# One core, a sequence layer with learned memory and routing: all steps of all stages in another order

## What is computed

```python
k, v, q = (causal_dwconv(hidden @ W.T, cw, cb) for W in (Wk, Wv, Wq))
alpha, eta, theta = gates(hidden)                       # one number each per token
for c0 in range(0, S, 128):                             # chunk by chunk
    g = grad(mem_loss)(W_state, k[c], v[c]) * 0.1       # pred = silu(k @ W1.T) @ W2.T
    g = g * min(1 / norm(g), 1)
    # per token: S = eta*S - theta*g;  W = (1-alpha)*W + S; W is kept for each token
    h = silu(q[c] @ W1t);  out[c] = h @ W2t
y = rmsnorm(out @ Wo.T) * norm_g * (hidden @ gW.T + gb)
x = layernorm(hidden + y)
x = layernorm(x + expert_w[argmax(x @ gate_w.T)] @ x)   # one of 8 experts per token
```

## Time and profile before

| | |
|---|---|
| median of 3 runs | 500.34 us (500.19 to 500.83) |
| span of the profiled execution | 498.6 us |
| PE busy | 435.3 us, 87% |
| weight loads of PE busy | 332.3 us, 67% |
| DVE busy | 392.7 us, 79% |
| ACT busy | 313.3 us, 63% |
| POOL busy | 274.6 us, 55% |
| mean granted clock of PE | 0.961 |

### The profile page before, as it was taken

One profiled execution on the slowest core, in us unless ns is written; L12 is line 12 of the kernel. 1 busy time (PEld: TensorE's weight loads), 2 busy tenths in 40 slices (PEclk: granted clock), 3 DMA queues, 4 the chain that ended last, 5 costly groups with the idle time before them and its releaser, 6 DMA issues.

```text
span 498.6 us, 11093 instructions
## 1 busy us (share of the span) xinstructions
PE 435.3 (87%) x3506; PEld 332.3 (67%) x3506; DVE 392.7 (79%) x1233; ACT 313.3 (63%) x791; POOL 274.6 (55%) x353
## 2 busy tenths in 40 slices
PE   6976999999999999899997989998679887996970
PEld 3654687767868677766866775866558776785750
...
GB/s 234 140 145 105 92 118 87 140 111 129 183 71 171 78 204 73 173 91 156 148 104 189 95 165 121 121 145 91 298 173 139 162 189 239 173 235 208 235 86 55
DMA packets 61353, 73.20 MB, mean 147 GB/s; under 512 B 17293, under 2 KB 48206, under 8 KB 61296
## 3 DMA queue, kind: packets, MB, share of 16 engines
...
## 4 chain that ended last, share of the span: by engine, by line
PE 35%; DMA 19%; DVE 16%; issue 10%; POOL 9%; ACT 9%; SPq 2%; POOLq 0%; DVEq 0%; ACTq 0%
DMA sorted_rows<-rows,index 7%; PE bank L523 6%; PE bank L624 5%; PE bank L1352 4%; DMA out<-os,xs_token 4%; POOL sorted_rows L1127 4%; ACT rows L1049 4%; DVE y L1007 3%; PE bank L544 3%; POOL index L1123 2%; DMA front<-sorted_rows 2%; DMA y<-in_hidden 2%; DVE kq_in L573 2%; ACT junk L990 2%; PE bank L1057 1%
## 5 line engine op out<-in xcount | busy, mean ns | idle before, releaser
L1127 POOL DMA_INDIRECT sorted_rows<-rows,index x64 | 77.0, 1203 | 27.0 <-issue 12.2
L1397 POOL DMA_INDIRECT out<-os,xs_token x71 | 70.1, 987 | 36.6 <-DVE mv L1026 14.1
L573 DVE SCALAR_TENSOR_TENSOR kq_in<-shared,conv_w,kq_in 128x256 f32<-128x256 f32 x144 | 60.7, 474 | 8.9 <-ACT kq_in L564 8.8
L523 PE MATMUL bank<-front 128*64 128x256 f32 x512 | 61.6, 394 | 6.8 <-DMA front<-in_w_kv 4.7
L624 PE MATMUL bank<-front 128*128 128x256 f32 x256 | 62.5, 388 | 0.7 <-DVE gt L629 0.7
L1352 PE MATMUL bank<-shared,front 128*128 x212 | 53.0, 394 | 5.3 <-ACT front L1331 1.8
L523 PEld LDWEIGHTS bank<-front 128*64 128x64 f32 x512 | 37.0, 141 | 26.5 <-DMA front<-in_hidden_t 5.7
L624 PEld LDWEIGHTS bank<-front 128*128 128x128 f32 x256 | 46.8, 193 | 8.8 <-issue 1.6
L1352 PEld LDWEIGHTS bank<-shared,front 128*128 128x128 f32 x212 | 39.4, 195 | 13.2 <-issue 8.5
L1049 ACT ACTIVATE rows<-y,rstd 128x256 f32<-128x256 f32 x64 | 34.0, 590 | 18.5 <-DMA sorted_rows<-rows,index 14.4
L1015 POOL DMA_DIRECT2D y<-in_hidden x16 | 16.1, 1007 | 35.7 <-DVE y L1007 27.8
...
## 6 DMA issues: line engine op xcount, KB each, us to landing
...
q<-kq_in SPq DMA_DIRECT2D x64, 64.0 KB, 2.9
...
hq<-hq SPq DMA_DIRECT2D x64, 64.0 KB, 2.6
shared<-in_w_expert SPq DMA_DIRECT2D x2, 1024.0 KB, 11.9
```

Source lines behind the costliest of these rows:

```text
L523: ins = pe.matmul(halves[half(side), kind, :, :], w[:, k, kind * D:(kind + 1) * D], pairs[:, k, side, :, :], start=k == 0, stop=k == KH - 1)
L573: dve.scalar_tensor_tensor(dst, raw[g][:, kind, :, tap:tap + P], conv_w[:, kind, tap:tap + 1], dst, ALU.mult, ALU.add))
L1127: pool.indirect_dma_start(sorted_rows[:, :], bass.IndirectOffsetOnAxis(index[i2][:, b:b + 1], 0), R[:, b, :], None, bounds_check=NE * REGI ...
L1397: pool.indirect_dma_start(out[:, :], bass.IndirectOffsetOnAxis(xs_token[t % LOADS][:, i:i + 1], 0), os_[o][:, i, :], None, bounds_check=TO ...
```

## The change

Only the text ORDER is another one. It has the same 2388 entries, each generator as often as before, in another sequence; products with the same cut of the array stand next to each other more often. No operation, buffer or wait is added or taken away. Of the text's lines, the first five and the three with the entries 1620 to 1799 (around the last projection, `pf`, and the load of the weights, `w0`):

```diff
 ORDER = (
-    "p0p0p0p0g0p1p0p0p0p0p0p0p0p0p0p0p0p1p0p0p0p1p0p0p0p1p0p1p0p0p1p1p1p1s0p1p1p1p1p1p1p1p1p1p1p1p0p1l0p0s0p1p1l0p2p0l0p1p1l0"
-    "p1p0l0s0p1s0s0l0s0s0p1l0s0l0l0s1l0s1p0p1l0l0s0l0s0l0l0l1p4s1l0l1s0l0s0p2p2s1p1p2p2p2p1l0s0p2p2s0p3s0p2p2s1p2p2p2s1p2p2p2"
-    "p2p2p2p2p2p1l1l1l1s0l0s2l0p2s1s1r0l1l1p2l1s2r0r0l1p2r0s2s1l1s2l1l1s1l1l1s1p2s2s1l2l1l1r0l1p2r0p3s2s2l1p3s2l2p3p3r0l1s1l1"
-    "p3s1r0p3p3p3s1l2p3p3p3p3p3p3p3p3p3p3p3p3l2r0p2p3p3l2r1s1l2l2p3e0s3l2r1l2r1e0p6e0p2p3p2e0s3p3l2l2s2e0l2e0l2e0s3r0r0s2e0l2"
-    "l2p3s2r1l2s3l3p3p3s2l3p4p3e0s3s3p4l2s2p4p4p4s2r1s2p5l2e0p4r1l3e0p4p4p4e0e0e0r1p4p4p4p4p4p4p4l3p4p3p4p4r0p4e0r1l3s3e0e0l3"
+    "p0p0p0p0p1p0g0p1p1p0p0p0p0p0p0p0p1p1p0p0p0p0p0p0p0p0p1p0p1p1p1p1p1p1p1l0l0p1p0p1l0p1p1p1p1p1p1p1p0p0p0p0s1l0l0p1p0l0s1p0"
+    "s0l0l0p1p0s0l0s1l0p1l0l0l0l0p1s0l0p1p1p1l1s0l0p3s0l1l0s0p2p2p2s1p1s0p2s0p2s0p2l0s1p2s0l1p2p2s0s0p2p2p2p4p2p2p2p2p2s1p2p2"
+    "p2l1p2l1s0p2s0p2p1p1p2l0p2l1s0l0l1p2p2l1l1p2r0l0l1l1s1p2l1r0l1l1s0s2l2s1l1s2s1s1s1l1r0s1s1r0l2r0r0p3p3p3l1p3s2l1l1l1p3p3"
+    "p3s2r0p3l2p3p3p3p3p3p3s1p3p3p3p3p3s2p3s1p3r1l2r0p3e0r1p3l2r1e0e0l2s1p3l2s3r1l2s3s2e0e0l2l2s2e0p3r0e0l2l2r0p3e0l2l2s3s2p3"
+    "s2l3p3e0p6r1r1s2p4s2l3r1l2l2p4s2p3l2s3p4p4e0e0p4p5l2e0p4e0e0p4p4l3e0p4p3p3s3p4r1p4p4p4p4p4p4r0p4p4p4l3s2s2p4l3e0s2e0s3r1"
 ...
-    "pfpfebpfecpeecrdseleebecpfrdpelepfpfealepfseealfebecebecececleecselfeasfebebserdebpfeblfserdleseebleebpfeblerdealepeleec"
-    "lfpfsfeapflfw0ebebealfebeblfebsfleebebebebpfrdebeblesfecpfy0y0sfy0pfeceby0rdecpfedecedecpfecpfley0ecebedy0edpfsfececlfec"
-    "ecy0leedlelfecsfeblflfededrerex0edlfeclfecedx0x0ecw0lfx1w0ecsfsfrex0sfecx1x1eclfx2sflfx2x1x2x2x0x3x1x1x2sfx3ededededx1ec"
+    "leebrdecpfpfeardrdeaeaecpfpfseebebrdeblepfeaebebpepflfecececececpflesepeecpflfseeaeblfpfebebebrdebseleebebseleleleebebrd"
+    "lesflfeblfeblfebebpfebpfrdebebleebebsflflfy0pfrdpelepfsflfsfecececy0ececy0sfebsflfpfpfrdpfecw0edlfecebebedy0y0pfecedy0pf"
+    "ecy0edlfleeclex0edececx0lex0reededx0lfedsfedw0ecececw0x1eclfedecx1sfreecsfsfx2rex1ecsfx2x2ecx1x2edecedecx0ececedx1x2x3x1"
 ...
```

More of the change, by code:

```diff
@@ L1429 @@
[L1429 to L1444, removed]
@@ L1453 @@
[L1453 to L1456, removed]
@@ new lines @@
+    "r1l2l2e0s2l3e0l3s4e0p4p4p4l3r1s3e0e0e0p4e0e0e0s3r1l3r2e0s4l3r0l3r2p4l3e0e0l3r2e1e0r0l3s3r2s3s3e1e1s4e1s3s4l4s4l3e0l3e1e1"
+    "l3e1e0l3l3r2r2e1s3p5p5p5l4l3p5e0p5r2p5p5e1p5p5l4p5p4p5p5s3e0p5p5p5e0l4s3p5p5p5p5l4s3p5r2p5l4s4p4r3r2p4e2e0l4s5p5l4l4e2e1"
+    "p5e1l4p5r3e2p5r1s4e1p5r3s5e1l4e1e0l4l4r1e0s4e0e1e2r3p5s5p5l4r2l4l5l5s4e1e1p7s4l4l4e1s4l4s4r2s5s4p6e1p5e1s4p6p6r2l5s5p6e2"
+    "p6l5s4p6p6p6p6r3e2e2e2e2p5p6p6r3p6p6p6p6p6r3p6p6p6p5l4p6s5l4p6e1e1p6e1l5p6e1l5p6s6l5l5l5e1p6r3r4r3e1s5r4r2l5e1l5r4s4e1l5"
@@ new lines @@
+    "l5r3l5s6e0s5e2r2e1e2l6e2e0e3l5e1e2e2l6r3s5e3l5e3s5r4p7e2s5e2p7e2e2s5e3l5e2e2s6r3l5e1s6s6p7l5e1l6s6p7r4e3r4e3l6l6e3e3s5e3"
+    "l6p7e2p7e1e2p7e1r4p6p7p8e1l5e1l6p7e2p7p9p7p7s6p7p7p7l6e1r3p7p7s5e2l6p6e1p7p7e2p7r5r3e2s5e1p7l6p7s5r4s7r5p7e3s7l6l6l6p7e2"
+    "r4e3p6r5r5l6p7e3e2e3e1e2e3s6p7p7p7s7p7e1s6r4e2e3s7e4r4l6e4s6s6e3l6r5e2s6s7r5p8e4r5s6e2e3e3e3s6e4r4e3p8e4l6e4p8e4l7p8e4p8"
+    "l7p7p8p8e2e2p7e3l6p8s6l6l7e2p8s7p8l6e2p8p8e4e3e3p8p8s7l7e2p8p8p8p8e2p8p8p8p8p8r5l7s7r6l7e3e3r6l7l7r6s7e3l7p8r5p8e2e3r5e2"
@@ new lines @@
+    "l7r5l7l7e3e3r4e4r6s7l7e5e2r4e4e4l7s8e3s7s6e4s8e5p8e5e4s8s8s7l8e3e3p8e4s8l7p9p8e4l8l7r6s8p9e4e5l7l7s7r5e4e4e4l8pce5e5e5p9"
+    "p9p9r6e5e3l7p9e5e3l7p9e4p9e3p9r6s7e4pal8p9s8p9e3p9p9p9p9p9e4p9p9p9p9p9e4s7r6r7p9e3l8l8p9e4r6r5e3p9e4s7r7l8r7e4p9s9l8l8s8"
+    "e5p9pdp9e3l8e5p9l8r5e4e5l8r7e5l8r6e3l8e4l8e5s8l9s9p9l8r6s9e3e6l9s8r6e5s8s9r7l8e4l8e6e4r7e5e6pae5s8e5l9e5e5pas8e6pas9e6e6"
+    "l9e6pae4e6l9papbe4papae6s8pap9e4p9r7l8e4pal9s9pae4pae4l8e5pae5papapapapapal9e6s9e5e6par7pae5e4par8pae5r7par6papae4pae6r8"
@@ new lines @@
+    "l9e5s8e5r8s8r7e5e5r7r6e5e6r8l9pas9l9l9l9l9l9l9e6s9s9e5e4e4s9e5s9l9e6e7r7e7s9e7s9e6e6r8e7r8sae6r8lal9e6pbe6sapbl9lapbe7e7"
+    "pbpbe7sae7salapbsal9pbe5e7pbe5lae5l9e5s9pbe5e5pblapbpblar7e5pbpbsapbpbpbe6pbpblapbs9e6e6pbpbpbe7pblae6e6lasar7lar8e5e6pa"
+    "e7r9e6pbe7pblae5pbe6lae7e6r8e7pbsbr9lar9sae6r8r8sbe8sapbe7lae8sasae6lar9pbe8lbsasbe7e8pclae7e7sbsalae7e7lasapcsbpbsbe8pc"
+    "pce8e8e8e6pclar9e6e8lbe7r9e6lae6e6e6e6e6pclbsapcpcpcr9pce6pcpcpcpcpcpcpcsapcpcpcr8e7lblblbe7r9lbsbe7e6rae7lbe8pcralbscr9"
@@ new lines @@
+    "e7r9e7ralbpcpclbsclbsbpcr8lbe8e7ralbe7e8e8e8lbr8pcr9sbscsce9sce8e9lbe9e8e9sbsbrarasbr9e7lce8sclbe8lbpde8e8e7pde7pdpdlbe9"
+    "pde9sce9e9lce7e9lbpde7pde7e7pcpde8lcpde8rapdpdlce8lcpde8lcrapdpdpdlce8pdpdpde8pdr9lce8e9e7pde9e8pde9e8sbe7e7pcpdpde9pde9"
+    "rae8e7eapclce7rbpdsce8pde9sbear9rbeasclcpde9rbscearasclce9e9e9lce9pdeaeapeeae9e9easde8lce9lceasclcsblde8e8rapee8e9e8sbld"
+    "rbscpepelcrblce9ldrbe9sdpdeaperbldpeldrapesdpee8sde8e9easdldlde9sde9eaeapde9e8e8peeapepepepepepepee8pepepelcperbrapeldpe"
@@ new lines @@
+    "x2x4x0x2eeefeex2x1eex2eex1x3x2x2efx2x4eeefefedx2x0efefefx2x4x3x4eex0efx1x3x0eex4x2x4m0x1x3x4x2x3eex2x3x3x2x1x2eex1m0x4x4"
+    "eeeeeeeex4eex2eex3x4x2eeeex3eex4m0eex1x4eex2x2eex4x4x1eeefx1x1efefx2een0efx2x0x0x0efx3x2efx1efm0x2x1efx2m0x2efx2efx2efx4"
+    "x2x3efx1x4x2efeex1eex0efn0x3n0n0x2x3efx2x1x4efx4x3efx4efefx3efx3efx1efefx1n0efx2x2x4x0eex4x4x4x1efefefx2efx2x2x3x3efefx2"
+    "efx1x1x4x2x3x2z0x2x0x4efx4n0efn0x2x4x1x3n0x1z0x3x2x0x4x2x2x2x3x0x2z0x2x4x2z0x4x2x0x2x4x2x2x3z0x3x1z0x2z0x4z0x4z0x4x2x3x1"
@@ L1461 @@
+    "x2x1x0x3x1x0x2x2x4x4x2x4x4x3x1x2x4x1x4x2x1x3x2x0x2x3x2x2x1x4x2x1x4x2x2x4x1x3x0x3x2x2x1x0x3x2x3x3x4x2x4x4x2x4x2x3x4x4x3x3"
+    "x4x4x1x2x2x1x1x2x4x0x0x4x2x2x1x2x1x4x1x2x4x2x2x3x4x2x3x1x1x0x4x4x3x1x4x3x2x2x0x2x3x4x2x2x2x1x3x4x2x1x3x1x3x4x2x2x4x1x3x3"
+    "x4x2x4x4x1x2x2x2x0x4x4x2x2x2x4x2x4x2x3x1x4x1x2x3x2x3x3x2x4x2x4x4x4x3x4x2x4x4x3x4x2x2x3x4x3x4x4x4"
 )
```

18 lines of the change are left out of this document (6 added, 12 removed).

## The result

The changed kernel takes 484.73 us (median of 4 runs, 481.82 to 487.46) where the kernel before takes 500.58 (500.19 to 502.78): a ratio of 0.971, 95% interval 0.967 to 0.975. By the medians that is 15.9 us faster, by the ratio some 14.6. The forecast was 494.6, so the direction is right, the size is not: the time lies under the range. The profiled execution of the changed kernel took 484.91 us, with a span of 483.7; its mean granted clock is 0.958, against 0.961 before, so the gain is not that of a higher clock.

What follows compares the result with a forecast made beforehand. PE paces up to 330 us, then POOL's store queue sets the last 119 us; -4.2 (cut changes) -2.0 (start) +0.5 (weights) = -5.7 us gives 494.6 us, range 488.0 to 501.0.

Steps and rivals of the forecast that it cites:

- changes of the cut: Places in PE's order where the tile shape of the array changes: 47 fewer, counted as 4.2 us saved.
- the price of a change: On PE, each change of the array's cut costs 0.09 to 0.10 us: 4.2 to 4.7 us for 47.
- The hand-over: At 330 to 378 us, the expert weights' load moves behind carry_t.15: cost 0 to 1.6 us, taken as 0.5.
- The start: PE's 4.27 us wait ahead of zq.0, near 45 us: 2.0 us won, range -0.4 to 7.5.
- Covers elsewhere: Work between producer and consumer in one queue, chiefly norm_h to grad_w on DVE: counted as zero, other end 4 us.
- rival 1: The forecast itself: 494.6 us, give or take 4 us for shorter or longer covers; chance 0.57.
- Rival 3: No change, 500.3 us: saved PE time in the middle stretch turns into PE waiting for DVE; chance 0.14.
- Rival 4: Slower, up to 505.6 us: expert weights in SP's queue arrive late and delay the first output store; chance 0.17.

Runs made afterwards that it cites:

- the added products: 32 small products cutting the array unlike their neighbours, added to the kernel before: 509.91 us, against 504.15 us with the neighbours' cut.

## Why the prediction was off

**Right.** The end is the first output store plus 120 us, in both kernels. The direction is right, and so is the count of the changes of the cut: of the 47 saved, 46 lie ahead of the first expert product. Products of lines 820 and 713 still follow each other at the two spacings, in the changed kernel too:

```profile
225.60 0.38 PE L820 MATMUL bank<-ident,e_t 128*128 128x128 f32 x2
225.92 0.72 PE L713 MATMUL bank<-kq_in 64*128 64x128 f32 x8
226.47 1.03 PE L980 MATMUL bank<-w_o,ret 64*128 64x256 f32 x8
...
264.75 0.38 PE L820 MATMUL bank<-ident,e_t 128*128 128x128 f32 x2
264.97 1.89 PE L624 MATMUL bank<-front 128*128 128x256 f32 x8
...
267.98 0.61 PE L713 MATMUL bank<-kq_in 64*128 64x128 f32 x8
```

For line 820 it is 0.32 us ahead of another cut and 0.22 ahead of the same.

**Mis-sized: the price of a change.** These spacings are one side of it only. The row of line 713 at 225.92 shows the other: behind another cut its eight products take 0.72 us, and the next line follows after 0.55 us although it has the same cut (0.44 us in the earlier trace rows). The prediction read the eight products of line 713 only where they stand behind line 980, which has their own cut, and so missed it. With both sides the 46 changes are some 7.8 us by the estimate of 0.17 us for each, and not the 4.2 to 4.7 us of the prediction. The estimate of 53 ns from the Trainium skill's page "TensorE: Matmul & The Clock Gate" (Part 2, on the drain) is too small by these rows and by the 0.13 to 0.14 us of the added products.

**The hand-over.** The load started right behind carry_t of unit 15, as worked out; it landed after 6.8 us (median) instead of the 11.9 taken from before, so the additions ended at 355.0, 1.7 us ahead of the first expert product, and the 0.5 us fell away. The rest of the 2.4 us won at the hand-over has a row for one part: PE's 2.08 us in front of the second turned tile. It was named, but not put into the sum, and not tested.

**The start.** PE's wait of 4.27 us ahead of line 782 went, and the clock in 44 to 52 us is 1.00 as forecast. A lead of 2.9 us at unit 4 answers to the 2.0 plus five changes of the cut (0.9 us); as the 2.0 was picked out of -0.4 to 7.5, that it fits is in part luck. And the lead did not last: the wait at 88.7 us took it all and more, so that at unit 9, with 26 changes of the cut or some 4.4 us saved, the changed kernel is only 0.2 us ahead. The step did not ask what the new order puts in PE's way later.

**The step that failed is "Covers elsewhere".** It was counted as zero, with one more wait of 4 us as its other end and "give or take 4 us" in rival 1; the gain was larger than that. It followed one stretch, norm_h to grad_w, counted DVE's instructions in it, and left out those of POOL, although the wait listed there is a wait for POOL. In the old order a load of y, a step on the counts, the index and two scatters stand in POOL's queue between the norm of unit 10 and its weight; in the new order a single small step does. That was to be counted in the order's text before any run. And ACT's 11.1 us of waiting for scatters, the first entry of ACT's waits in this stretch, was not looked at, because ACT is busy for only two thirds of it. Both waits ended in PE, whose idle time between units 9 and 15 fell from 9.5 to 3.0 us: 6.5 us where the sum had nothing. Lifted in the old order, they took that idle time down to 4.0 us and shortened the stretch by 4.7 to 6.4 us.

**What that leaves of the 12.3 us.** Of the 5.8 us by which PE's busy time fell, 2.0 us are ten products (a gate product of line 624 in eight pieces, two transposes of line 782) that lie outside this stretch in the new order, and 22 changes of the cut at their two-sided price are 3.7 us. With the 6.5 us of idle time that makes 12.2 us. That it comes so near is in part luck: PE's wait at unit 10's projection was 1.30 us in one execution and 0.30 in two others whose order is the same up to there, and the granted clock was 0.99 instead of 1.00 in the changed kernel.

**The rivals.** Rival 3 put PE's idle time in the middle at over 16 us: it is 10.6. The Trainium skill's page "Trainium Kernel Development and Optimization", section Performance Expectations, calls matmul busy time a bad measure and the busy share of the weight loads a good one. The prediction read from it that a quarter of PE was free and that nothing was to be won; here that share even rose from 73% to 76% (203.85 of 270 us) and the time fell by 3%, so the measurement decides against that reading. Rival 4, the weights as the late transfer, did not come: the additions did wait, 2.06 us, but under cover. The busy time of PE fell by 8.5 us and not by 4, which is near the two-sided price of the changes; but 2.8 us of it are the expert products of line 1352, whose ends are modelled, so that this proves nothing by itself.
